# Channel attention in a fused gated layer stack: the bias products of the projections moved to 32 rows of the array, behind a slot's scores

## The chip, the cores and the metric

The kernel runs on one core of a Trainium2 chip. The metric is the device time of one execution, in microseconds. A core has a matmul engine (TensorE, PE in the profile, with its weight loads shown apart as PEld), three engines for elementwise work (VectorE or DVE, ScalarE or ACT, GpSimd or POOL) and a queue engine for transfers (SyncE or SP). Matmuls write to PSUM, eight banks of 128 partitions by 2 KB; the other engines read them there.

## The reference

A stack of layers works on x (16 batches, 128 tokens, 256 features). The first layer, the only one that the change touches, is a cross attention over channels, with 16 heads of size 8:

```python
q = einsum('oc,bct->bot', Wq, target) + bq      # 128 x 256 for each batch
k = einsum('oc,bcs->bos', Wk, source) + bk
v = einsum('oc,bcs->bos', Wv, source) + bv
dot = einsum('bhdt,bhds->bhts', q, k) / sqrt(8)
mask = target_mask[:, :, :, None] * source_mask[:, :, None, :]
dot = mask * dot - (1.0 - mask) * NEG
amap = softmax(dot, axis=-1) * mask
out = einsum('bhts,bhds->bhdt', amap, v)
```

Behind it come a feed-forward layer with ternary weights, two attentions over tokens, and a layer of routed experts. All of it is float32.

## The kernel before

`attend_channels` is the first stage, up to about 340 us of the execution. The other stages follow in blocks of their own.

**Layout.** A projection gives for each head 32 rows: the 8 rows of q (or k) three times, for a product in high and low parts, and a few rows that carry bias and mask terms. Four heads fill 128 partitions, so a head's scores contract over 32 rows only: partitions 32r to 32r+31, row group r. q and k of a batch are 512 rows each, made in two pieces of 256 (`part` 0 and 1), each piece in one PSUM bank (`proj`, two banks taken in turn) as two halves j of 128 x 256. v is one piece. So a batch has five pieces, q0, q1, k0, k1, v0.

**A piece.** `project` (L831) makes each half with four matmuls over the full array: the bias product, whose operands `bext` (bias rows) and `mext` (mask rows) are zero but for 4 of their 128 partitions (0 to 3), and three with high and low parts of weights and input. `project_v` (L849) does the same with the operands' roles exchanged. `freed` makes the piece wait until the piece two back has left its bank. ScalarE then rounds the piece out of its bank (`round_piece`, L744), and VectorE stacks the result (`stack_piece`, L1010), which frees the bank.

**Slots.** The order of all engines is written out by slots t; u = t mod 16. In slot t the first pass takes head u of batch t // 16: `first` (L872), two matmuls of 32 rows by 128 columns by 256, then VectorE's row maxima (L1019). The second pass runs 24 slots later: `second` (L892), two such matmuls with the maxima folded in, then ScalarE's exponential (L774). `first` of slot u uses row group u mod 4, `second` of the same slot group (u + 2) mod 4. In the stream of PE the two are interleaved: first 0, second 0, first 1, second 1. `first` waits for a free bank of three (the maxima of some slots before), `second` for one of two banks (the exponential of two slots before) and, at the first head of a batch, for the maxima that come back by DMA (L597).

At u = 0, 4, 8, 12 and 13 PE then makes a piece of the next batch (`built`, `PIECES`), at u = 2, 6, 10, 14 it weighs the values (`weigh`, L922, 128 rows by 32 columns), and at u = 2 it turns the maxima (L902). In the slots before 24 there is no second pass, and PE has other products of a later stage between (L151). In the slots -16 to -1 there are no scores at all, only batch 0's pieces. From slot 240 on no pieces are left.

ScalarE's order in a slot: the exponential, then at u = 2 the maxima (L760), at u = 1, 5, 9, 13 a piece's rounding, at 14 v (L750), at 0 a normalisation for a later batch (L727), at 3 the mask (L766), at 3 and 11 the outputs (L782).

Of the kernel before, what the change touches and what calls it, by code (L numbers as in the profile page):

```python
# [7 lines left out]
F32 = mybir.dt.float32  # L8
# [7 lines left out]
P = 128  # L16
# [350 lines left out]
def attend_channels(nc, res, io, gate, work, tern):  # L367

    x_sb, ident = res["x"], res["ident"]
    with ExitStack() as stack:  # L370
# [39 lines left out]
        mT = s.sb("mT", [A_HEADS, 2, DIM], F32R)  # L410
        PR = 8
        prob = s.sb("prob", [P, PR, 2, DIM])
        early = prob[0:4, :, :, :].rearrange("p a t n -> p (a t n)")
        braw, bhi = early[:, 0:1152], early[:, 1152:2304].bitcast(F32R)
        osb = s.sb("osb", [P, 2, A_TILES, DIM])
        num, den = (wraw[:, 512 * k:512 * k + 512].rearrange("p (b n) -> p b n", b=2) for k in range(2))
# [48 lines left out]
        def turned(t):  # L465

            b = t // U - 1
            return b if t % U == 2 and 0 <= b < BATCHES else None
# [27 lines left out]
        def prepared(t):  # L496

            b = t // U + 2
            return b if 2 <= b < BATCHES else None

        PIECES = {0: ("q", 0), 4: ("q", 1), 8: ("k", 0), 12: ("k", 1), 13: ("v", 0)}
        WARM = 40
        MEASURED, CONDENSED = 4, 17
# [67 lines left out]
        with nc.Block() as block:  # L571

            @block.sync
            def _(sp):
                lo, rest = slice(0, FIRST), slice(FIRST, BATCHES)
                sp.dma_start(x_sb[:, lo, :], io["x"][lo].rearrange("b p n -> p b n")).then_inc(ld_x[0], 16)
                sp.dma_start(wraw[:, 0:512], io["a_wq4"]).then_inc(ld_w, 16)
                sp.dma_start(wraw[:, 512:1024], io["a_wk4"]).then_inc(ld_w, 16)
                sp.dma_start(wraw[:, 1024:1152], io["a_wv"]).then_inc(ld_w, 16)
                sp.dma_start(cst[:, :], io["a_consts"]).then_inc(ld_w, 16)  # L580
                sp.dma_start(g[:, :], gate.broadcast_to([P, 1])).then_inc(ld_g, 16)
                sp.wait_ge(m_parts, 1)
                sp.wait_ge(blank_ext, 2)
                for k in range(4):
                    sp.dma_start(mext[k:k + 1, :].rearrange("o (b n) -> o b n", n=DIM).bitcast(F32),
                                 mparts[BATCHES * k:BATCHES * k + BATCHES, :].bitcast(F32)).then_inc(m_ext, 16)
                work.fetch(sp, 0)
                sp.dma_start(x_sb[:, rest, :], io["x"][rest].rearrange("b p n -> p b n")).then_inc(ld_x[1], 16)
                sp.dma_start(ctx_sb[:, rest, :], io["ctx"][rest].rearrange("b p n -> p b n")).then_inc(ld_c[1], 16)
                sp.dma_start(tm[:, rest, :].rearrange("p b n -> p (b n)"),  # L590
                             io["mask"][:, FIRST * DIM:].broadcast_to([P, (BATCHES - FIRST) * DIM])).then_inc(ld_m[1], 16)

                def maxima(b):
                    sp.wait_ge(mT_ready, b + 1)
                    for r in range(A_SLOTS):
                        row = A_ROWS * r + 27
                        sp.dma_start(qs[row:row + 1, b % A_BUFS, :, :].bitcast(F32),  # L597
                                     mT[A_TILES * r:A_TILES * r + A_TILES, b % 2, :].bitcast(F32))\
                            .then_inc(m_in[b % 2], 16)

                def gather(b):
                    p, i = b % 2, b // 2
                    sp.wait_ge(out_copied, 2 * b + 2)
                    if b >= 2:
                        sp.wait_ge(moved[p], 32 * i)
                    send(sp, p, 0)
                    if b < BATCHES - 1:
                        send(sp, p, 1)
                    sp.wait_ge(sent[p], 128 * (i + 1))
                    after(sp, x_done, 3 * (b - 1))  # L610
                    sp.dma_start(num[:, p, :], heads[p, 0]).then_inc(moved[p], 16)
                    if b < BATCHES - 1:
                        sp.dma_start(den[:, p, :], heads[p, 1]).then_inc(moved[p], 16)

                maxima(0)
                maxima(1)
                for b in range(BATCHES):
                    gather(b)
                    if b + 2 < BATCHES:
                        maxima(b + 2)  # L620
                    if b == 10:
                        sp.wait_ge(cm_ready, BATCHES)
                        work.fetch(sp, 1)
                    if b == 12:
                        sp.wait_ge(v_psum, BATCHES)
                        sp.wait_ge(tgm_ready, 14)
                        tern.load(sp)
# [197 lines left out]

            @block.tensor
            def _(pe):
                def project(b, kind, part, j):
                    psum_s, k = (q_psum, 0) if kind == "q" else (k_psum, 1)
                    h, l = ((xh, xl), (ch, cl))[k]  # L830
                    if j == 0:  # L831
                        freed(pe, b, kind, part)
                        pe.wait_ge((xl_ready, cl_ready)[k], b + 1)
                        if b == 0 and k == 0 and part == 0:
                            pe.wait_ge(w_lo, 1)
                            pe.wait_ge(b_ext, 1)
                            pe.wait_ge(m_ext, 64)
                    c = 512 * k + P * (2 * part + j)
                    w = slice(c, c + P)
                    o = proj[bank_of(b, kind, part)][:, j, :]  # L840
                    pe.matmul(o, bext[:, w], mext[:, DIM * b:DIM * b + DIM], start=True, stop=False)
                    pe.matmul(o, wh[:, w], h[:, b % 2, :], start=False, stop=False)
                    pe.matmul(o, wh[:, w], l[:, b % 2, :], start=False, stop=False)
                    mm = pe.matmul(o, wl[:, w], h[:, b % 2, :], start=False, stop=True)
                    if j == 1:
                        mm.then_inc(psum_s, 1)

                def project_v(b):
                    freed(pe, b, "v", 0)  # L849
                    w = slice(1024, 1152)  # L850
                    for t in range(2):
                        c = slice(P * t, P * t + P)
                        o = proj[bank_of(b, "v", 0)][:, t, 0:P]
                        pe.matmul(o, mext[:, DIM * b + P * t:DIM * b + P * t + P], bext[:, w], start=True, stop=False)
                        pe.matmul(o, ch[:, b % 2, c], wh[:, w], start=False, stop=False)
                        pe.matmul(o, ch[:, b % 2, c], wl[:, w], start=False, stop=False)
                        mm = pe.matmul(o, cl[:, b % 2, c], wh[:, w], start=False, stop=True)
                    mm.then_inc(v_psum, 1)

                def first(b, u, t):  # L860
# [74 lines left out]
                for t in SLOTS:  # L935
                    one, two = unit1(t), unit2(t)
                    for c in range(2):
                        if one:
                            first(*one, c)
                        if two:  # L940
                            second(*two, c)
                    if turned(t) is not None:
                        turn_maxima(turned(t))
                    if weighed(t):
                        weigh(*weighed(t))
                    u, b = t % U, built(t)
                    if b is not None:
                        if u in (0, 4, 8, 12):
                            project(b, *PIECES[u], 0)
                            project(b, *PIECES[u], 1)  # L950
                        if u == 13:
                            project_v(b)
                    if t in SUMMED:
                        pe.wait_ge(mT_ready, BATCHES)
                        tern.weight_sum(pe, SUMMED.index(t), side)
                    if t == TURNED:
                        tern.turn_scale(pe, 0, tern.sparts, scales, tern.FIRST, ident)
                    i, turns = gram_of(t)
                    for h in turns:
                        if h == 0:  # L960
                            gram_room(i)
                        work.multiply(pe, i, h, gram_bank[i])
# [5 lines left out]
            def _(dve):  # L968
# [11 lines left out]
                def mean_bias(a, b, k):  # L980
# [16 lines left out]
                dve.wait_ge(b_hi, 1)  # L997
                dve.wait_ge(ld_b, 16)
                dve.wait_ge(blank_ext, 2)
                dve.scalar_tensor_tensor(bext[0:4, :], bhi[:, :].bitcast(F32), ecst[0:4, 0:1], braw[:, :],  # L1000
                                         ALU.mult, ALU.add).then_inc(b_ext, 1)
                dve.wait_ge(vT_blank, 1)
                dve.memset(vT[:, :, :, :, A_HD:2 * A_HD], 1.0).then_inc(ones_set, 1)
# [2622 lines left out]
def lay_out(inputs):  # L3626
# [26 lines left out]
    bv[:3] = f["L0_xattn_bv"]  # L3653
    out["a_bias"] = np.concatenate([rows.reshape(4, -1), bv], 1)
    out["a_econsts"] = np.zeros((4 * BATCHES, 2), np.float32)
    out["a_econsts"][2, 0] = out["a_econsts"][BATCHES:2 * BATCHES, 1] = -1.0
    c = np.zeros((A_ROWS, 2), np.float32)
    c[[*range(16, 24), 26], 0] = -1.0
    c[[*range(8, 16), 25], 1] = -1.0
# [82 lines left out]
```

## Time and profile before

| | |
|---|---|
| median of 3 runs | 1811.39 us (1809.07 to 1817.93) |
| the profiled execution | 1818.41 us, its span 1816.6 us |
| busy, share of the span | PE 95%, PEld 80%, DVE 63%, ACT 54%, POOL 29% |
| mean granted clock of TensorE | 0.967 |
| the stage that changes | to about 340 us; pieces under scores from 28 to 275 us |

Times in the profile are microseconds from the start of the span. A matmul's row in the timeline has its start, its duration, the line, then output<-inputs, rows*columns of the array and the shape (partitions x elements). Durations overlap, since matmuls are pipelined; the distance between starts is what one costs in a stream. A matmul that has to wait for its own weights starts with their load. Rows that follow each other closely with the same line are merged (x2, x4).

### The profile page before, as it was taken

How to read it: one execution, taken by the hardware profiler on the slowest of the kernel's cores; microseconds unless marked ns; L12 is line 12 of the kernel's file. 1: busy time of each engine (PE TensorE's matmuls, PEld its weight loads, DVE VectorE, ACT ScalarE, POOL GpSimd, SP SyncE). 2: the span in 40 equal slices, each digit the busy share in tenths (PEclk: the TensorE clock that was granted, in tenths of full speed). 3: DMA queues.
4: the chain of work that ended last, by engine and by line, in shares of the span. 5: the costliest groups of instructions: out<-in, count | busy, mean ns of one | idle time of the engine just before them, and what ended most of it. 6: DMA issues, size and time to landing. Idle time of an engine off the chain costs nothing. (4 is left out here: it accounts for less than half of the span.)

```text
span 1816.6 us, 34407 instructions
## 1 busy us (share of the span) xinstructions
PE 1730.8 (95%) x11806; PEld 1449.5 (80%) x11814; DVE 1145.4 (63%) x2572; ACT 979.7 (54%) x2544; POOL 535.2 (29%) x578
## 2 busy tenths in 40 slices
PE   8999999698999999999999999999999998899997
PEld 6666665355888888888888888888888888789985
DVE  6788987687655656556556655555555566864434
ACT  2578886386554544454555555445445543755543
POOL 4233323153431211111112211111111211377773
PEclk9899998698999999999999999999999997999999
DMA  5011123012100100100001020101000004443447
GB/s 202 14 37 32 33 83 100 21 48 97 50 13 1 48 12 1 49 12 12 25 24 36 13 63 13 36 1 36 12 1 12 1 1 109 148 113 117 128 127 263
DMA packets 48775, 97.43 MB, mean 54 GB/s; under 512 B 7322, under 2 KB 29002, under 8 KB 47620
## 3 DMA queue, kind: packets, MB, share of 16 engines
q1 hardware_dynamic: 39807, 72.42, 13.1%
q0 software_dynamic: 7584, 21.37, 4.0%
q8 instruction: 104, 1.70, 0.4%
q10 hardware_dynamic: 1216, 1.41, 0.2%
q14 instruction: 64, 0.52, 0.1%
HBM read 73.85 MB, written 20.97 MB: 52 GB/s over the span
## 5 line engine op out<-in xcount | busy, mean ns | idle before, releaser
L2192 POOL TENSOR_TENSOR hold_wq<-hold_wq,ca_rsum 128x512 f32<-128x512 f32 x128 | 133.2, 1041 | 797.9 <-DVE ca_rsum L2434 797.9
L2046 ACT ACTIVATE hold_wq<-hold_wq,ca_nb,ca_evens 128x128 f32<-128x128 f32 x256 | 123.3, 483 | 227.5 <-DVE ca_nb L2429 227.5
L2046 ACT ACTIVATE hold_wq<-hold_wq,ca_nb,c_rqs 128x128 f32<-128x128 f32 x256 | 123.4, 483 | 225.8 <-DVE ca_nb L2429 225.8
L1019 DVE TENSOR_REDUCE a_mx<-a_s 128x2 f32<-128x512 f32 x256 | 166.4, 682 | 43.4 <-PE a_s L872 40.6
L774 ACT ACTIVATE a_prob<-a_s 128x512 f32<-128x512 f32 x256 | 147.8, 601 | 65.5 <-PE a_s L892 62.0
L2209 PE MATMUL ca_qk<-early_x,cw_wqkv_h 128*128 128x512 f32 x384 | 161.9, 422 | 1.0 <-PEq L1455 1.0
L2211 PE MATMUL ca_qk<-early_x,cw_wqkv_l 128*128 128x512 f32 x384 | 151.7, 395 | 0.0
L2210 PE MATMUL ca_qk<-early_x,cw_wqkv_h 128*128 128x512 f32 x384 | 151.2, 394 | 0.0
L2330 PE MATMUL ca_acc<-ca_wo_h,ca_oT_h 128*128 128x256 f32 x512 | 146.0, 285 | 0.0
L2331 PE MATMUL ca_acc<-ca_wo_l,ca_oT_h 128*128 128x256 f32 x512 | 145.0, 283 | 0.0
L2332 PE MATMUL ca_acc<-ca_wo_h,ca_oT_l 128*128 128x256 f32 x512 | 144.9, 283 | 0.0
L2252 PE MATMUL ca_s<-ca_qk 128*128 128x128 f32 x1024 | 135.7, 275 | 5.2 <-issue 5.2
L2271 PE MATMUL ca_oT<-hold_wq,ca_values 128*128 128x128 f32 x1024 | 136.1, 276 | 0.0
L2252 PEld LDWEIGHTS ca_s<-ca_qk 128*128 128x128 f32 x1024 | 125.3, 191 | 7.2 <-issue 7.0
L2434 DVE RECIPROCAL ca_rsum<-ca_sums 128x4 f32<-128x4 f32 x128 | 22.8, 178 | 167.3 <-ACT hold_wq L2046 167.3
L2271 PEld LDWEIGHTS ca_oT<-hold_wq,ca_values 128*128 128x128 f32 x1024 | 125.2, 193 | 0.0
L2424 DVE TENSOR_TENSOR hold_wq<-ca_s,hold_wk 128x512 f32<-128x512 f32 x128 | 88.1, 688 | 54.2 <-PE ca_s L2252 53.8
L892 PE MATMUL a_s<-a_qs,a_ks 32*128 32x256 f32 x512 | 102.6, 346 | 16.7 <-ACT a_prob L774 14.7
L2441 DVE SCALAR_TENSOR_TENSOR ca_oT_l<-ca_oT,ca_bv,ca_oT_h 128x512 fp32r<-128x512 f32 x64 | 48.1, 751 | 92.6 <-ACT ca_oT_h L2060 92.6
L2330 PEld LDWEIGHTS ca_acc<-ca_wo_h,ca_oT_h 128*128 128x128 f32 x512 | 97.7, 191 | 5.1 <-DVE ca_oT_l L2443 0.2
L2331 PEld LDWEIGHTS ca_acc<-ca_wo_l,ca_oT_h 128*128 128x128 f32 x512 | 97.4, 190 | 5.2
L2332 PEld LDWEIGHTS ca_acc<-ca_wo_h,ca_oT_l 128*128 128x128 f32 x512 | 97.4, 190 | 0.0
(526 smaller groups left out, 4893.0 us busy)
## 6 DMA issues: line engine op xcount, KB each, us to landing
early_big<-slot_results SPq DMA_DIRECT2D x16, 512.0 KB, 8.0
mw_raw<-in_d_expert_w SPq DMA_DIRECT2D x12, 352.0 KB, 5.3
a_heads<-a_osb SPq DMA_DIRECT2D x124, 32.0 KB
a_wraw<-a_heads SPq DMA_DIRECT2D x31, 128.0 KB, 2.1
mw_down<-in_d_expert_d SPq DMA_DIRECT2D x1, 2816.0 KB
token_rows<-early_rows SPq DMA_DIRECT2D x1, 2176.0 KB, 13.1
hold_wk<-in_c_wkT SPq DMA_DIRECT2D x1, 2064.0 KB
hold_wq<-in_c_wqT SPq DMA_DIRECT2D x1, 2064.0 KB, 8.0
```

What stands on the lines that cost most here:

```text
L774: act.activation(prob[:, w % PR, :, :], s2_bank(w)[:, :, :], ACT.Exp, scale=1.0 / A_ROOT)\
L1019: dve.tensor_reduce(mx[:, b % 2, :, h], s1_bank(b, u)[:, :, :], AX.X, ALU.max)\
L2046: ins = act.activation(prob[:, p, b, :], prob[:, p, b, :], ACT.Exp, bias=nb[:, p, b:b + 1], scale=row_scale[layer][:, r:r + 1], accum_out= ...
L2192: pool.tensor_tensor(prob[:, k % 2, :, :], prob[:, k % 2, :, :], rsum[:, k % 2, :].unsqueeze(2).broadcast_to([P, GB, TOKENS]), ALU.mult)\
L2209: pe.matmul(out, ah, bh, start=start, stop=False)
L2210: pe.matmul(out, ah, bl, start=False, stop=False)
L2211: return pe.matmul(out, al, bh, start=False, stop=stop)
L2252: mm = pe.matmul(s_ps[:, b, :], qk[:, p, 0, tok], qk[:, p, 1, tok], start=True, stop=True)
L2271: mm = pe.matmul(oT_ps[:, b, :], v[:, g_ % 2, b, c], pT[:, p, b, :], start=True, stop=True)
L2330: pe.matmul(acc[:, b, :], ah, bh, start=(h == 0 and b % 2 == 0), stop=False, skip_group_check=True)
L2331: pe.matmul(acc[:, b, :], ah, bl, start=False, stop=False, skip_group_check=True)
L2332: mm = pe.matmul(acc[:, b, :], al, bh, start=False, stop=(h == 3), skip_group_check=True)
```

## The change

The bias products leave `project` and `project_v`. A new function `bias` makes both of a piece's bias products directly behind the slot's scores, ahead of anything else of the slot. Its operands lie in partitions 32 to 35, and the matmuls read 32 partitions (32 to 63, row group 1) instead of 128: the form of the scores. The first of the two opens the accumulation for the whole bank (`start`), the second and the six matmuls of the piece add to it. The wait for the bank (`freed`) goes with them, ahead of the bias products; the wait for the low part of the input stays ahead of the six. The rest moves the operands: `bext`, `mext`, the bias constants and the scratch rows `early` go from partitions 0 to 3 to partitions 32 to 35.

```diff
-        early = prob[0:4, :, :, :].rearrange("p a t n -> p (a t n)")
+        early = prob[A_ROWS:A_ROWS + 4, :, :, :].rearrange("p a t n -> p (a t n)")
...
+        EXT = slice(A_ROWS, 2 * A_ROWS)
...
-                    sp.dma_start(mext[k:k + 1, :].rearrange("o (b n) -> o b n", n=DIM).bitcast(F32),
+                    sp.dma_start(mext[A_ROWS + k:A_ROWS + k + 1, :].rearrange("o (b n) -> o b n", n=DIM).bitcast(F32),
...
+                def bias(b, kind, part):
+                    freed(pe, b, kind, part)
+                    if b == 0 and kind == "q" and part == 0:
+                        pe.wait_ge(b_ext, 1)
+                        pe.wait_ge(m_ext, 64)
+                    o = proj[bank_of(b, kind, part)]
+                    for j in range(2):
+                        if kind == "v":
+                            pe.matmul(o[:, j, 0:P], mext[EXT, DIM * b + P * j:DIM * b + P * j + P], bext[EXT, 1024:1152],
+                                      start=(j == 0), stop=False, skip_group_check=True)
+                        else:
+                            c = 512 * (kind == "k") + P * (2 * part + j)
+                            pe.matmul(o[:, j, :], bext[EXT, c:c + P], mext[EXT, DIM * b:DIM * b + DIM],
+                                      start=(j == 0), stop=False, skip_group_check=True)
...
                 def project(b, kind, part, j):
...
                     if j == 0:
-                        freed(pe, b, kind, part)
                         pe.wait_ge((xl_ready, cl_ready)[k], b + 1)
                         if b == 0 and k == 0 and part == 0:
                             pe.wait_ge(w_lo, 1)
-                            pe.wait_ge(b_ext, 1)
-                            pe.wait_ge(m_ext, 64)
...
-                    pe.matmul(o, bext[:, w], mext[:, DIM * b:DIM * b + DIM], start=True, stop=False)
-                    pe.matmul(o, wh[:, w], h[:, b % 2, :], start=False, stop=False)
-                    pe.matmul(o, wh[:, w], l[:, b % 2, :], start=False, stop=False)
-                    mm = pe.matmul(o, wl[:, w], h[:, b % 2, :], start=False, stop=True)
+                    pe.matmul(o, wh[:, w], h[:, b % 2, :], start=False, stop=False, skip_group_check=True)
+                    pe.matmul(o, wh[:, w], l[:, b % 2, :], start=False, stop=False, skip_group_check=True)
+                    mm = pe.matmul(o, wl[:, w], h[:, b % 2, :], start=False, stop=True, skip_group_check=True)
...
                 def project_v(b):
-                    freed(pe, b, "v", 0)
...
-                        pe.matmul(o, mext[:, DIM * b + P * t:DIM * b + P * t + P], bext[:, w], start=True, stop=False)
...
+                    u, b = t % U, built(t)
+                    if b is not None and u in PIECES:
+                        bias(b, *PIECES[u])
                     if turned(t) is not None:
                         turn_maxima(turned(t))
                     if weighed(t):
                         weigh(*weighed(t))
-                    u, b = t % U, built(t)
```

## Rows read from the trace of the kernel before

**Rows 1.** The page: busy time, share of the span and instructions.

```profile
PE 1730.8 (95%) x11806; PEld 1449.5 (80%) x11814; DVE 1145.4 (63%) x2572; ACT 979.7 (54%) x2544; POOL 535.2 (29%) x578
```

**Rows 2.** Windows: length, busy of each engine, granted clock, DMA.

```profile
58.70:72.40 13.70, 13.70 (x91) 9.07 (x90) 6.38 (x10) 5.93 (x12) 3.55 (x6) 0.50 0.01 2
88.60:104.50 15.90, 15.52 (x171) 10.57 (x170) 14.25 (x23) 12.99 (x27) 5.67 (x10) 1.00 0.16 36
```

**Rows 3.** Waits, 27 to 300 us: us in total, times, longest.

```profile
ACT a_prob L774 <- PE a_s L892: 58.1, 87, 2.5
```

**Rows 4.** Timeline of PE, slot 12: last scores, piece k1, next scores.

```profile
111.69 0.38 PE L892 MATMUL a_s<-a_qs,a_ks 32*128 32x256 f32 x1 [0.25 <-ACT a_prob L774]
...
111.91 0.28 PE L892 MATMUL a_s<-a_qs,a_ks 32*128 32x256 f32 x1
112.11 0.39 PE L841 MATMUL a_proj<-a_mext,a_bext 128*128 128x256 f32 x1
112.34 0.28 PE L842 MATMUL a_proj<-a_ch,a_wh 128*128 128x256 f32 x1
112.45 0.27 PE L843 MATMUL a_proj<-a_cl,a_wh 128*128 128x256 f32 x1
...
113.04 0.28 PE L844 MATMUL a_proj<-a_ch,a_wl 128*128 128x256 f32 x1
113.25 0.38 PE L872 MATMUL a_s<-a_ks,a_qs 32*128 32x256 f32 x1
```

**Rows 5.** Timeline of PE, slots 15 and 0, and piece q0.

```profile
116.15 0.38 PE L872 MATMUL a_s<-a_ks,a_qs 32*128 32x256 f32 x1
...
116.17 0.38 PE L892 MATMUL a_s<-a_qs,a_ks 32*128 32x256 f32 x1
116.38 0.28 PE L872 MATMUL a_s<-a_ks,a_qs 32*128 32x256 f32 x1
...
116.39 0.28 PE L892 MATMUL a_s<-a_qs,a_ks 32*128 32x256 f32 x1
116.66 0.39 PE L841 MATMUL a_proj<-a_mext,a_bext 128*128 128x256 f32 x1
```

**Rows 6.** Timeline of PE: `second` of slot 25, `first` of slot 27, both group 3.

```profile
56.26 0.28 PE L892 MATMUL a_s<-a_qs,a_ks 32*128 32x256 f32 x1
...
56.38 0.27 PE L872 MATMUL a_s<-a_ks,a_qs 32*128 32x256 f32 x1
```

**Rows 7.** Timeline of PE, slots 7 and 8, and piece k0.

```profile
107.72 0.38 PE L892 MATMUL a_s<-a_qs,a_ks 32*128 32x256 f32 x1
...
107.94 0.36 PE L892 MATMUL a_s<-a_qs,a_ks 32*128 32x256 f32 x2
...
108.14 0.27 PE L892 MATMUL a_s<-a_qs,a_ks 32*128 32x256 f32 x1
108.34 0.39 PE L841 MATMUL a_proj<-a_mext,a_bext 128*128 128x256 f32 x1
```

**Rows 8.** Timeline of ScalarE, slots 15 to 6.

```profile
117.69 0.60 ACT L727 ACTIVATE a_xn<-x_sb,a_nbias,a_rstd 128x256 f32<-128x256 f32 x1
118.37 0.60 ACT L774 ACTIVATE a_prob<-a_s 128x512 f32<-128x512 f32 x1
118.87 0.59 ACT L744 ACTIVATE a_hi<-a_proj 128x512 fp32r<-128x512 f32 x1
...
121.55 1.19 ACT L774 ACTIVATE a_prob<-a_s 128x512 f32<-128x512 f32 x2
```

**Rows 9.** Timeline of PE's weight loads, slot 6.

```profile
122.20 0.18 PEld L892 LDWEIGHTS a_s<-a_qs,a_ks 32*128 32x128 f32 x1 [0.33 <-ACT a_prob L774]
```

**Rows 10.** Timeline of VectorE: two stacks that free a bank.

```profile
24.32 0.75 DVE L1010 SCALAR_TENSOR_TENSOR a_qs<-a_hi,a_cst,a_proj 128x512 fp32r<-128x512 f32 x1 [0.89 <-ACT a_hi L744]
...
115.87 0.74 DVE L1010 SCALAR_TENSOR_TENSOR a_ks<-a_hi,a_cst,a_proj 128x512 fp32r<-128x512 f32 x1
```

**Rows 11.** The tile a_proj, 27 to 300 us: duration ns min/median/max, first and last start.

```profile
L841 PE MATMUL a_proj<-a_mext,a_bext x120: 278/382/581, 28.1 to 272.9; 128*128 128x256 f32 x120
```

More of the change, by code:

```diff
@@ L853, in project_v @@
                         o = proj[bank_of(b, "v", 0)][:, t, 0:P]
-                        pe.matmul(o, mext[:, DIM * b + P * t:DIM * b + P * t + P], bext[:, w], start=True, stop=False)
-                        pe.matmul(o, ch[:, b % 2, c], wh[:, w], start=False, stop=False)
-                        pe.matmul(o, ch[:, b % 2, c], wl[:, w], start=False, stop=False)
-                        mm = pe.matmul(o, cl[:, b % 2, c], wh[:, w], start=False, stop=True)
+                        pe.matmul(o, ch[:, b % 2, c], wh[:, w], start=False, stop=False, skip_group_check=True)
+                        pe.matmul(o, ch[:, b % 2, c], wl[:, w], start=False, stop=False, skip_group_check=True)
+                        mm = pe.matmul(o, cl[:, b % 2, c], wh[:, w], start=False, stop=True, skip_group_check=True)
                     mm.then_inc(v_psum, 1)
@@ L999, in _ @@
                 dve.wait_ge(blank_ext, 2)
-                dve.scalar_tensor_tensor(bext[0:4, :], bhi[:, :].bitcast(F32), ecst[0:4, 0:1], braw[:, :],
+                dve.scalar_tensor_tensor(bext[A_ROWS:A_ROWS + 4, :], bhi[:, :].bitcast(F32),
+                                         ecst[A_ROWS:A_ROWS + 4, 0:1], braw[:, :],
                                          ALU.mult, ALU.add).then_inc(b_ext, 1)
@@ L3655, in lay_out @@
     out["a_econsts"] = np.zeros((4 * BATCHES, 2), np.float32)
-    out["a_econsts"][2, 0] = out["a_econsts"][BATCHES:2 * BATCHES, 1] = -1.0
+    out["a_econsts"][A_ROWS + 2, 0] = out["a_econsts"][BATCHES:2 * BATCHES, 1] = -1.0
     c = np.zeros((A_ROWS, 2), np.float32)
```

## The prediction

> **What bounds the kernel now.** First the page's busy times: TensorE's matmuls fill 95% of the span [rows 1], so the first question is what its stream loses in the stage that changes. That stage is the channel attention, 27 to 340 us. Second, the stretch by stretch table [rows 2]: in one batch period (15.9 us at the full clock, 16 slots) PE is busy 15.52 us, VectorE 14.25 and ScalarE 12.99. All three are close to full, so a matmul saved counts only where PE is the one that the others wait for at that moment. Third, the waits [rows 3]: ScalarE waits 58.1 us in this stage for scores (L892 to L774), 87 times, so there are such moments, about six in a period. Fourth, the order of single instructions around each projection piece, which says at which of the five pieces of a period that is so.
>
> The full-array piece, at slot 12 (k, part 1) [rows 4]: scores at 111.69 and 111.91, first projection matmul (the bias product, L841) at 112.11, the next at 112.34, the third at 112.45, the eighth at 113.04, the next scores at 113.25. So: from the last 32-row score to the first full-array matmul 0.20 us; first to second 0.22 (the weights of the first are loaded in the open); each further one 0.12; back to the scores 0.21. The two bias products of a piece are two links of 0.12 in this chain.
>
> **What the change takes away.** In each q or k piece eight full-array matmuls become six: 2 x 0.12 = 0.24 us less. The exposed first weight load stays, because L842 then stands first. In the v piece likewise two links, of about 0.11 us. There are no more switches between the 32-row form and the full array than before where scores stand ahead of the piece, since bias products now follow scores in the scores' form and no other matmul comes between.
>
> **What it adds.** Two 32-row matmuls in row group 1 (partitions 32 to 63). What they cost is a question of which row groups are busy. At slots 0, 4, 8 and 12 the slot's own scores use groups 0 and 2, and the slot before used groups 3 and 1 (its `second` sits in group 1). At slot 13 `first` uses group 1 itself.
>
> Do row groups run beside each other, and out of the program's order? The tight case, slots 15 and 0 [rows 5]: eight scores, four start at 116.15 to 116.17, four at 116.38 to 116.39. In the program the second half of slot 15 (same row groups as its first half) stands ahead of the first half of slot 0; if starts kept the order, slot 0 could not start beside slot 15. So a row group is a line of its own: 0.22 us from its first matmul after a break to its second, and 0.12 to a third behind it (56.26 to 56.38, group 3) [rows 6].
>
> The Trainium skill says otherwise (PSUM — Partial Sum Buffer, section Engine vs sequencer instructions): matmuls "start and complete in program order", with only weight loads pulled ahead. This trace doesn't agree for starts in different row groups, by the four starts within 0.02 us. By the page's rule the total below would be near -0.5 us, by the rows -4.4; it is rival B.
>
> Now the five pieces of a period:
>
> - Slot 12. The scores of slot 12 come late, behind the exponential (0.25 us idle), at 111.69 and 111.91 [rows 4]; group 1 has long been empty. The two bias products are issued behind them and run beside them. Cost 0 in the forecast, 0.12 if starts keep their order. Net -0.24. On the path: ScalarE and VectorE wait for slot 13's scores.
> - Slot 8. Scores of slot 7 in group 1 at 107.72 and 107.94, the last score of slot 8 at 108.14, bias at 108.34 [rows 7]. Bias products at 107.94 + 0.12 = 108.06 and 108.18, projection at 108.18 + 0.20 = 108.38 in place of 108.34: +0.04. Net -0.20. On the path, as slot 9's scores are what ScalarE waits for next.
> - Slot 4. As slot 12: -0.24 on PE. But behind it ScalarE is in an unbroken run, from 118.37 on to the pair of exponentials at 121.55, and PE itself then waits 0.33 us for it, at 122.20 [rows 8, 9]. The gain turns into a longer wait there. Worth 0.
> - Slot 0. The piece waits for its bank, which VectorE's stack of k (L1010) frees at 115.87 + 0.74 = 116.61 [rows 10]; the bias product starts 0.05 later, at 116.66, and not 0.20 behind the last score (116.39) but 0.27 [rows 5]. After the change this wait stands ahead of the 32-row pair, which has nothing left to hide behind: pair 0.22 (first start to second), 0.20 for the switch, so the projection starts 0.42 later, less 0.24: net +0.18. On the path: the exponential at 118.37 waits for slot 1's scores, while the operation before it (L727, 117.69) would let ScalarE on 0.48 after its start, some 0.2 us earlier (its usual pace: 0.50 from the exponential at 118.37 to the operation behind it) [rows 8].
> - Slot 13, v. Group 1 holds two scores of its own; third and fourth matmul in it cost 2 x 0.12, two links of 0.11 are saved: 0.
>
> Sum of a period: +0.18 - 0.20 - 0.24 = -0.26 us. Twelve periods look like this (slot 0 pieces from 84.84 to 260.98 us): -3.1 us.
>
> Ahead of them, 27 to 81 us (the bias products of the q and k pieces under scores run from 28.1 to 272.9, 120 of them, two to a piece [rows 11]): only first-pass scores run up to 54 us, group 1 is free at slots 0, 4, 8, 12, so a piece gains 0.24. I count five such pieces on the path (28.14, 31.84, 40.82, 50.75, 54.89): -1.2; one hidden behind VectorE (35.98): 0; one that waits for VectorE (45.84): +0.2. The one at 58.66 falls where the clock is half [rows 2] and a link about twice 0.12: -0.4. Of the next, two tight ones give 0 (66.56, 72.42), then -0.1 and -0.24 (76.52, 80.29). Together -1.75.
>
> The opening, 19.8 to 27.7 us: batch 0's pieces have no scores ahead of them. There the change does add switches: k part 1 starts at 25.12 because VectorE's stack of q (24.32 + 0.75) frees its bank [rows 10]. As at slot 0 the pair then stands alone, +0.18; the same for k part 0 and v. The bias product of q part 0 moves ahead of the wait for the lowered x and gains 0.4, which the new switches of q part 1 take back. Together +0.5.
>
> Other edits: operands at partitions 32 to 35 in place of 0 to 3 have the same sizes, so VectorE's and ScalarE's instructions and the four DMAs into the mask rows cost what they cost; they end by about 18 us, ahead of the first projection at 19.87. If that cover were gone they would move the opening one to one.
>
> By the Trainium skill (TensorEngine Tiling (Array Packing), section Key Properties) a change of the tiling mode drains the array. The trace agrees: 0.20 in place of 0.12. By that rule too the two bounds of a piece differ only in whether a switch is added, which happens in the opening alone.
>
> **Sum.** -3.1 - 1.75 + 0.5 = -4.4 us, all within the stage; behind it the stages follow one another, so it reaches the end one to one. The profiled execution took 1818.4 us (span 1816.6 and 1.8 around it) and would take 1814.0. It was 7.0 us above the median of the runs, 1811.39. I carry the difference, not the level: 1811.4 - 4.4 = 1807.0. The three runs lie 8.9 us apart, so about 0.5% (9.06 us) is what can be told from no change.
>
> **Rivals.**
>
> A, all the PE time counts. ScalarE's run at slots 1 to 6 gives way too, and the pair at slot 0 hides: 12 x 3 x 0.24 + 1.75 = 10.4 less, and the opening's loss hidden too: 1801.0, 0.57% faster. For it: PE's 95% [rows 1]. Against it: PE's own wait at 122.20 [rows 9].
>
> B, starts keep the program's order (the page's rule). The pair then ends 0.12 behind the last score: slot 12 -0.12, slot 8 about -0.11, slot 0 still +0.18; a period -0.05, twelve of them -0.6; ahead of them six times -0.12 and +0.2; opening +0.5. About -0.6: 1810.8.
>
> C, the slower side: the clock. The granted clock is 0.50 in 58.7 to 72.4, behind two waits of PE for the exponentials, and 1.00 through the batch periods [rows 2]. At 0.50 it issued 91 matmuls in 13.7 us; at 1.00 171 take 15.9, so 91 take 8.5: a stretch costs 5.2 us. Each period loses 10 full-array matmuls of some 171 and gets longer waits at slots 4 to 6. If the clock fell in these periods it would take three more such stretches to undo 4.4 and cost over 9: (9.06 + 4.4) / 5.2 = 2.6. With three: 1822.6. Against: periods with 0.33 us waits and gaps held 1.00.
>
> D, the pair never overlaps: 0.24 each, so pieces break even, and slot 0 and the opening lose: 12 x 0.18 + 0.2 + 0.5 = +2.9: 1814.3. It would need group 1 to be blocked by the other groups, which [rows 5] speaks against.
>
> **Chances and range.** Forecast 0.50, A 0.13, B 0.16, C 0.09, D 0.12. The likeliest one's own range is 1803 to 1811. From 1801 (A's value) to 1816 (D with a run's scatter) 0.8 and a bit lies; outside are most of C, and A where it scatters lower. Faster by over 0.5%: A, with a little of the forecast's scatter, 0.14; slower by over 0.5%: C, 0.08; within: 0.78.
>
> **What would show it.** In the changed trace: six full-array matmuls per piece, piece length 0.90 in place of 1.14. At slot 12 two 32-row bias matmuls that start with the scores, and 0.20 from the last score to the projection; at slot 8 some 0.04 later than now; at slot 0 bias products 0.05 behind VectorE's stack and the projection 0.42 behind their first. The wait at 122.20 grows to about 0.5. Period 15.65 us in place of 15.9. Wrong it would be if bias products start only behind the last score (B), if the periods shrink by 0.7 (A), or if the granted clock has new stretches of 0.50 (C), which could also hide or double the gain by where the stretch at 58.7 falls.

## The result: slower by 0.6%, with a stage that gains where it was forecast and loses its clock where it was not

The changed kernel's median is 1824.51 us (20 runs, 1811.55 to 1832.93), that of the kernel before 1812.8 (20 runs, 1807.0 to 1817.93): ratio 1.0062, 95% interval 1.0049 to 1.0076. Forecast were 1807.0 us and a range of 1801 to 1816. The profiled execution took 1832.93 us, span 1831.0. It is the slowest of the 20: the comparison of the two traces shows what the change does to the clock at its fullest, the medians what it costs in general.

The page of the changed kernel first, part 1 and the clock's row of part 2 (each digit a fortieth of the span, 46 us), then the clock's row of the kernel before:

```profile
PE 1743.4 (95%) x11806; PEld 1453.3 (79%) x11814; DVE 1149.3 (63%) x2572; ACT 979.0 (53%) x2544; POOL 533.5 (29%) x578
PEclk6599999688999999999999999999999997899999
```
```profile
PEclk9899998698999999999999999999999997999999
```

The same number of matmuls (x11806, as in [rows 1]), shares that agree within a point, and two lower digits at the very start. The windows of the changed kernel say how long that lasts (columns as in [rows 2]):

```profile
20.00:25.00 5.00, 4.92 (x17) 4.02 (x18) 1.04 (x2) 1.19 (x2) 3.58 (x7) 0.50 1.10 351
...
30.00:40.00 10.00, 10.00 (x37) 6.79 (x36) 4.41 (x8) 2.07 (x4) 3.56 (x6) 0.50 0.04 17
...
16.20:91.30 75.10, 71.31 (x288) 48.57 (x288) 39.66 (x78) 18.13 (x36) 18.30 (x28) 0.50 0.20 73
91.30:104.50 13.20, 12.55 (x147) 8.43 (x139) 10.33 (x17) 10.00 (x21) 0.82 (x2) 1.00 0.12 22
```

and the same windows of the kernel before:

```profile
20.00:25.00 5.00, 5.00 (x24) 4.87 (x24) 1.43 (x2) 1.20 (x2) 3.35 (x6) 0.54 1.10 349
...
30.00:40.00 10.00, 9.79 (x51) 6.29 (x51) 9.40 (x19) 1.20 (x2) 2.38 (x5) 1.00 0.04 14
```

Before, the granted clock is 0.50 (1.2 GHz) from 17.8 to 24.6 us, rises to 1.00 (2.4 GHz) in the opening, and falls once more among the pieces, from 58.8 to 72.4. After, it is 0.50 from 16.2 to 91.3 us without a break. Behind the last piece both fall again (301.1 to 338.6 and 316.6 to 343.9 us); all that lies behind it changes the difference of the two spans by 0.4 us only (below).

The first fall is there in both: PE has nothing to do from 13.7 us (13.0 in the changed kernel) until the opening's first matmul, and the clock falls within that gap. What brings it back in the kernel before is the opening. Its q0 and q1 are 16 full-array matmuls on end, about 0.21 us apart; here are the first and the last:

```profile
19.87 0.58 PE L841 MATMUL a_proj<-a_mext,a_bext 128*128 128x256 f32 x1 [6.15 <-POOL a_xl L652]
...
23.24 0.41 PE L844 MATMUL a_proj<-a_xh,a_wl 128*128 128x256 f32 x1
```

Two places divide the two traces into three parts. The last matmul of the v piece of slot 45 starts at 82.70 before and 101.92 after, the last of the stage's last piece at 274.75 and 289.56 (in this order, before's two and after's two):

```profile
82.70 0.27 PE L857 MATMUL a_proj<-a_wh,a_cl 128*128 128x128 f32 x1
...
274.75 0.27 PE L857 MATMUL a_proj<-a_wh,a_cl 128*128 128x128 f32 x1
```
```profile
101.92 0.27 PE L867 MATMUL a_proj<-a_wh,a_cl 128*128 128x128 f32 x1
...
289.56 0.28 PE L867 MATMUL a_proj<-a_wh,a_cl 128*128 128x128 f32 x1
```

So +19.2 us up to slot 45 (forecast: -1.75 + 0.5, with a little more of it behind 82 us), then -4.4 us in the twelve periods (forecast -3.1), together +14.8; the spans differ by 14.4. The periods gained more than I said. The stretch ahead of them has 75.1 us at half rate against 6.8 + 13.7 = 20.5, so 54.6 us more. If its other terms came to the -1.25 of the forecast, the clock took 19.2 + 1.25 = 20.5 us, 0.37 us for each us at 0.50. My price, 5.2 us for 13.7, was 0.38.

**The pieces, one by one**, in the changed kernel's timeline of PE. Slot 8 (L902 is `second`, L882 `first`, L841 the bias product, L854 the first projection matmul):

```profile
189.84 0.39 PE L902 MATMUL a_s<-a_qs,a_ks 32*128 32x256 f32 x2
...
189.96 0.29 PE L841 MATMUL a_proj<-a_mext,a_bext 32*128 32x256 f32 x1
190.08 0.28 PE L902 MATMUL a_s<-a_qs,a_ks 32*128 32x256 f32 x1
190.09 0.27 PE L841 MATMUL a_proj<-a_mext,a_bext 32*128 32x256 f32 x1
190.29 0.38 PE L854 MATMUL a_proj<-a_ch,a_wh 128*128 128x256 f32 x1
...
191.19 0.38 PE L882 MATMUL a_s<-a_ks,a_qs 32*128 32x256 f32 x1
```

The first bias product starts at 189.96, ahead of the slot's last score at 190.08, which stands ahead of it in the program; the projection starts 0.21 behind that score, as if the pair weren't there. Piece 0.90 instead of 1.15. From the last score to the next scores it is 1.11 us (190.08 to 191.19), where it was 1.35 (108.14 in [rows 7] to 109.49): -0.24, where I had -0.20. Slot 12:

```profile
193.39 0.38 PE L902 MATMUL a_s<-a_qs,a_ks 32*128 32x256 f32 x1
...
193.40 0.38 PE L841 MATMUL a_proj<-a_mext,a_bext 32*128 32x256 f32 x1
193.61 0.27 PE L902 MATMUL a_s<-a_qs,a_ks 32*128 32x256 f32 x1
193.62 0.28 PE L841 MATMUL a_proj<-a_mext,a_bext 32*128 32x256 f32 x1
193.83 0.38 PE L854 MATMUL a_proj<-a_ch,a_wh 128*128 128x256 f32 x1
...
194.74 0.38 PE L882 MATMUL a_s<-a_ks,a_qs 32*128 32x256 f32 x1
```

The pair runs with the scores, 0.01 behind each. From the last score to the next scores it is 1.13 us, where it was 1.34 (111.91 to 113.25 in [rows 4]): -0.21. Slot 0, where VectorE's stack (first fence) frees the bank (PSUM is read here by VectorE and ScalarE, not by every engine):

```profile
197.30 0.74 DVE L1023 SCALAR_TENSOR_TENSOR a_ks<-a_hi,a_cst,a_proj 128x512 fp32r<-128x512 f32 x1
```
```profile
182.94 0.39 PE L854 MATMUL a_proj<-a_xh,a_wh 128*128 128x256 f32 x1
...
198.09 0.50 PE L841 MATMUL a_proj<-a_mext,a_bext 32*128 32x256 f32 x2
198.52 0.39 PE L854 MATMUL a_proj<-a_xh,a_wh 128*128 128x256 f32 x1
```

The stack ends at 198.04, the pair starts 0.05 later, the projection 0.43 behind it (forecast 0.42). From 182.94 to 198.52 is a period: 15.58 us, where it was 15.91. And slot 6, which waits for the exponential, in the weight loads' timeline:

```profile
188.19 0.18 PEld L902 LDWEIGHTS a_s<-a_qs,a_ks 32*128 32x128 f32 x1 [0.51 <-ACT a_prob L775]
```

0.51 us, where [rows 9] had 0.33: most of slot 4's gain has become a wait.

**The opening**, changed kernel, clock at 0.50:

```profile
21.32 0.41 PE L856 MATMUL a_proj<-a_xh,a_wl 128*128 128x256 f32 x1
21.67 0.79 PE L841 MATMUL a_proj<-a_mext,a_bext 32*128 32x256 f32 x2
22.39 0.58 PE L854 MATMUL a_proj<-a_xh,a_wh 128*128 128x256 f32 x1
22.77 0.41 PE L855 MATMUL a_proj<-a_xl,a_wh 128*128 128x256 f32 x1
```

Six full-array matmuls, then 21.32 to 22.39, 1.07 us, of a switch (to the 32-row form), the pair and a switch back, and so on between all pieces. Before, the 16 of q0 and q1 were unbroken. That is the trace's hint at the cause. A hint is all it is: the changed kernel is also short of ten full-array matmuls there, and has 32-row pairs in slots 0 to 31, and each of these could be what keeps the clock down.

### The profile page after: what moved, and what is told of

Its sections match the earlier page's. It is cut to its first block and busy times, and to the rows that moved or that the text cites. A ratio compares the mean times of both kernels' runs of the same rounds, so it can differ in the third digit from the quotient of the medians.

```text
span 1831.0 us, 34345 instructions
## 1 busy us (share of the span) xinstructions
PE 1743.4 (95%) x11806; PEld 1453.3 (79%) x11814; DVE 1149.3 (63%) x2572; ACT 979.0 (53%) x2544; POOL 533.5 (29%) x578
## 5 line engine op out<-in xcount | busy, mean ns | idle before, releaser
L902 PE MATMUL a_s<-a_qs,a_ks 32*128 32x256 f32 x512 | 104.8, 348 | 15.6 <-ACT a_prob L775 14.1
L882 PE MATMUL a_s<-a_ks,a_qs 32*128 32x256 f32 x512 | 103.3, 361 | 0.0
```

## The experiments

Most of them share one edit to the changed kernel, and differ in its condition:

```diff
                 def bias(b, kind, part):
                     freed(pe, b, kind, part)
...
+                    rows = EXT if CONDITION else slice(0, P)
                     o = proj[bank_of(b, kind, part)]
...
-                            pe.matmul(o[:, j, :], bext[EXT, c:c + P], mext[EXT, DIM * b:DIM * b + DIM],
+                            pe.matmul(o[:, j, :], bext[rows, c:c + P], mext[rows, DIM * b:DIM * b + DIM],
```

Where the condition doesn't hold, the bias products stand at the new place but use the full array. Ratios are against the kernel before on the same chip (its medians there 1810.99, 1811.25 and 1811.94 us in the three groups of four). Times are medians; a ratio is worked out from the runs of the two kernels taken together and can differ a little from the quotient of two medians. Windows quoted below are the runs' profiled executions, columns as in [rows 2]; the first of the last three numbers is the granted clock. A table behind the runs has the stretches of 0.50 of each trace and the mean clock of all executions.

**e1_open_full**, condition `b > 0`.

> The changed kernel, but batch 0's five pieces (the opening, no scores ahead of them) take their bias products over the full array again; all other pieces keep the 32-row pair. Theory T1: in the changed kernel the opening no longer brings the granted clock back to 1.00 at 24.6 us (it stays 0.50 from 16.2 to 91.3), because the change breaks the unbroken run of full-array matmuls there; the batch periods themselves gain (15.58 us in place of 15.91). Then the clock rises near 24.6 us here, the stretch of 0.50 up to 91 us is gone, and the time is 4 to 6 us below the kernel before: ratio 0.997 to 0.998. Rival T2: the 32-row pairs behind the scores, from 28 us on, keep the clock low; then the clock stays 0.50 to about 90 us here too and the ratio is near 1.006. Rival T3: both places matter: the clock rises at 24.6 but falls again between 28 and 80 us for longer than before's 13.7 us; ratio 0.999 to 1.004.

Measured: 1806.35 us, ratio 0.9978 (0.9955 to 1.0001).

```profile
25.00:30.00 5.00, 4.96 (x31) 3.85 (x31) 2.88 (x4) 2.07 (x5) 1.93 (x4) 1.00 1.07 409
...
40.00:60.00 20.00, 20.00 (x68) 13.55 (x66) 11.29 (x32) 3.04 (x6) 5.74 (x7) 0.50 0.01 2
```

The clock rose at 23.0 us, as T1 said. In the profiled execution (1813.43 us, one of the slower of its ten) it fell again from 40.1 to 81.1, which T1 did not say and T3 did; the ratio is in T1's range and below T3's. It is -4.0 us (-8.1 to +0.2) for everything outside the opening, where the prediction had -3.1 - 1.75 = -4.9.

**e2_open_only**, condition `b == 0`: the opening alone has pairs.

> The converse: only batch 0's pieces use 32 rows; the bias products of all other pieces stand at the new place, but over the full array (the pair, then six matmuls, eight in one run). T1: the clock stays 0.50 from about 17 us on, well past 58 us; ratio 1.005 to 1.012, as the gain of the periods is missing too. T2: the clock rises near 24.6 us as before; ratio 0.999 to 1.001. T3: rises, but somewhat later than 24.6; ratio about 1.002 to 1.005.

Measured: 1820.17 us, ratio 1.0064 (1.0043 to 1.0085). This is +11.6 us (7.8 to 15.4; 9.2 by the medians) for five pairs in the opening, where the prediction had +0.5. The whole change costs 11.2 by its ratio, but has the gains of the periods in it, which e2 has not.

```profile
20.00:25.00 5.00, 4.71 (x17) 3.81 (x17) 0.83 (x2) 1.19 (x2) 3.77 (x7) 0.50 1.10 352
...
30.00:40.00 10.00, 10.00 (x36) 7.45 (x36) 4.62 (x8) 1.47 (x3) 3.54 (x6) 0.50 0.04 15
```

0.50 from 17.3 to 41.2 in the trace, a run of 1813.53 us and a mean clock of 0.971; its other nine took 1811 to 1826 us at 0.963 to 0.972, so how long the clock stays down varies from execution to execution. The ratio is in T1's range, and T2 falls. That the clock would stay down well past 58 us, as T1 had it, this trace doesn't show.

**e3_after_warm** and **e4_before_warm**: `WARM` 66 in place of 40 (the identity products that fill the time ahead of the first piece), in the changed kernel and in the one before.

```diff
-        WARM = 40
+        WARM = 66
```

> The changed kernel with 66 in place of 40 idle-time transposes of the identity ahead of the first piece, so that the array is in use up to about 18.9 us and the clock should still be 1.00 when the opening begins. T1 (the clock is the loss, not the pairs): with the clock at 1.00 through the opening the time falls to 4 to 8 us below the kernel before, ratio 0.995 to 0.998. T2: the clock falls between 28 and 90 us all the same; ratio 1.003 to 1.006. T3: rises or holds at first, falls at about 58 us for some 14 us as before; ratio 0.996 to 1.000.

> The kernel before with the same 66. It shows what the filled gap alone brings: all theories expect the first stretch of 0.50 (17.8 to 24.6 us) to vanish, worth at most 3 us, ratio 0.998 to 1.000. The difference between this and the changed kernel with 66 is the change at equal clock: by my terms -0.26 to -0.33 us in twelve periods and -1.75 ahead of them, 4 to 5 us; by T2 the changed one stays slower.

Measured: the changed kernel 1811.6 us, ratio 1.0003 (0.9972 to 1.0034), its ten runs from 1800.97 to 1823.03; the kernel before 1807.03, ratio 0.9981 (0.9964 to 0.9998). In this order, 20 to 25 and 30 to 40 us of the changed one, then of the one before:

```profile
20.00:25.00 5.00, 4.74 (x22) 3.75 (x22) 1.49 (x2) 1.19 (x2) 3.71 (x7) 0.72 1.10 353
...
30.00:40.00 10.00, 10.00 (x34) 6.64 (x32) 4.89 (x8) 1.57 (x3) 3.55 (x6) 0.50 0.08 32
```
```profile
20.00:25.00 5.00, 4.11 (x32) 3.70 (x31) 2.10 (x3) 2.07 (x4) 3.28 (x6) 1.00 1.10 353
...
30.00:40.00 10.00, 9.79 (x52) 6.63 (x52) 9.77 (x20) 1.19 (x2) 1.00 (x2) 0.98 0.06 23
```

The stretch of 0.50 ahead of the opening is gone in both, as expected: it came from the gap. My expectation for the changed one, T1's ratio, was wrong. In its profiled execution (1822.81 us) the clock is 1.00 when the opening begins, and falls in it, at 22.2 us; before's opening holds it, and the clock falls at 39.5 us for 10 us. So in that trace an opening with pairs doesn't keep the clock. In other executions it seems to: five of the ten have a mean clock of 0.971 to 0.973 and took 1801 to 1811 us, the other five 0.960 to 0.966 and 1813 to 1823.

**e5_late_pairs**, condition `b > 2`, and **e6_late_pairs_q0_full**, condition `b > 2 and (kind, part) != ('q', 0)`.

> The changed kernel with full-array bias products for batches 0, 1 and 2, so in the opening and in slots 0 to 31; 32-row pairs only from slot 32 on. Where the first experiments stand: with the full-array form in the opening alone the clock rose at 23 us but was 0.50 again from 40.1 to 81.1; with 32 rows in the opening alone it was 0.50 from 17.3 to 41.2. Theory T3 (both places matter, because each takes full-array matmuls out of a stretch where the clock is near falling): here the stretches of 0.50 are those of the kernel before, about 18 to 25 and 59 to 72 us, the periods are 15.58 us each, and the ratio is 0.997 to 0.998. Rival (the clock is lost through the pairs in the batch periods too, or by chance): a low stretch of over 25 us between 40 and 100, ratio at or above 0.999.

> As the one before, and the first piece of each batch (q part 0, slot 0) keeps its bias products over the full array for all batches, since there the wait for the bank leaves the 32-row pair nothing to hide behind (0.43 us from its start to the projection, two links of 0.12 saved). By my terms 0.18 us a period: period 15.40 in place of 15.58, twelve or thirteen periods, 2.2 us less than the one before; ratio 0.996 to 0.997. Rival: slot 0's piece is not on the path, since ScalarE has a run of its own behind it: period stays 15.58.

Measured: 1808.92 us, ratio 0.9988 (0.9970 to 1.0006), stretches of 0.50 at 16.0 to 26.2 and 60.4 to 70.6; and 1804.96 us, ratio 0.9960 (0.9943 to 0.9976), stretches at 16.9 to 23.8 and 40.8 to 51.1. The first gained less than I expected, though the expected 0.998 lies within its interval; the stretches are about where they were before. The second is the test of slot 0: giving the pair up where it had nothing to hide behind brings the period from 15.58 to 15.43 us, 0.15, where my term was 0.18. Its rival, that slot 0 isn't on the path, falls.

**e7_pair_and_full** and **e8_neither**: for batches 0 to 2, both forms, or no bias product at all.

```diff
-                    for j in range(2):
+                    for rows, j in [(r, j) for r in ((EXT,) if b > 2 else (EXT, slice(0, P))) for j in range(2)]:
...
```

```diff
+                    if b <= 2:
+                        return
                     for j in range(2):
...
-                    pe.matmul(o, wh[:, w], h[:, b % 2, :], start=False, stop=False, skip_group_check=True)
+                    pe.matmul(o, wh[:, w], h[:, b % 2, :], start=(b <= 2), stop=False, skip_group_check=True)
```

> For batches 0, 1 and 2 both forms: the 32-row pair, whose result is thrown away (the full-array pair behind it opens the accumulation anew), and then the full run of eight. From slot 32 on as in the changed kernel. Ta, the clock is lost through the two full-array matmuls that each piece is short of: here none is missing, so the stretches of 0.50 are as with the full form alone, and only the pairs and switches cost, some 2 to 3 us; ratio 0.998 to 1.000. Tb, it is lost through the pair and its switches between the forms: the clock stays low to 40 us or longer, ratio 1.003 or more.

> Batches 0, 1 and 2 leave the bias products out altogether (their outputs lack bias and mask terms); from slot 32 on as in the changed kernel. Ta: six full-array matmuls in a row and nothing else, so the clock is lost as in the changed kernel: 0.50 for 24 us or more in all before 100 us, beyond the stretches of 18 to 25 and 59 to 72; ratio 1.000 to 1.006 although work is left out. Tb: no pairs and no added switches, so the clock is as before; ratio 0.996 to 0.998.

Measured: with both 1817.51 us, ratio 1.0026 (1.0004 to 1.0048); with neither 1802.84 us, ratio 0.9955 (0.9933 to 0.9978). First both, then neither:

```profile
20.00:25.00 5.00, 5.00 (x19) 4.10 (x19) 0.79 (x2) 1.19 (x2) 3.39 (x6) 0.50 1.10 350
...
30.00:40.00 10.00, 10.00 (x38) 7.33 (x38) 3.97 (x6) 1.84 (x4) 3.54 (x6) 0.50 0.04 16
```
```profile
20.00:25.00 5.00, 4.55 (x21) 4.14 (x22) 1.49 (x2) 1.53 (x3) 3.47 (x6) 0.60 1.10 349
...
30.00:40.00 10.00, 9.55 (x49) 6.05 (x49) 9.97 (x20) 1.19 (x2) 1.66 (x3) 1.00 0.04 14
```

With all full-array matmuls there and the 32-row pairs between them, the clock stays 0.50 from 15.2 to 42.5 us. With ten full-array matmuls fewer in the opening and nothing between the rest, it is 1.00 again at 24.0. Ta (matmuls missing) falls, Tb (the pair and its switches) stands. Both ratios miss Tb's narrowly (1.003 or more, 0.996 to 0.998). Which part of Tb does it, the small matmuls or the time that the switches take from the full-array ones, isn't shown: every run with the pairs has both. The busy column doesn't tell: PE is busy 5.00 of 5.00 us where the clock stays low and 4.55 where it rises.

**e9_first_pair_only**, condition `b > 0 or (kind, part) == ('q', 0)`, and **e10_four_pairs**, condition `b > 0 or (kind, part) != ('q', 0)`.

> In the opening only the first pair, that of q part 0, uses 32 rows (it stands ahead of the wait for x, some 1 us before the first projection); the other four pieces of batch 0 are full-array; from slot 0 on as in the changed kernel. What stands so far: the clock is lost where the opening's pieces have the pair and its switches between them, not where full-array matmuls are only missing. If it is the switches between pieces that keep the clock at 0.50 (Tb1), this one rises near 23 to 25 us, as q part 0 and 1 make an unbroken run of 14 full-array matmuls: ratio 0.996 to 0.999. If the pair's mere presence ahead of the run does it (Tb2), 0.50 lasts past 40 us, ratio 1.002 or more.

> The converse: q part 0 of batch 0 over the full array, the other four pieces of the opening with the 32-row pair. Tb1: the switches stand between all pieces, 0.50 from about 17 to past 40 us, ratio 1.004 to 1.008. Tb2: rises near 24 us, ratio 0.997 to 1.000.

Measured: 1807.79 us, ratio 0.9986 (0.9972 to 1.0000), the clock back at 23.9 us; and 1818.05 us (8 runs), ratio 1.0036 (1.0007 to 1.0065), a little under the 1.004 of Tb1, 0.50 from 17.9 to 69.1 and again from 75.9 to 93.0. A pair ahead of the run does no harm that these runs can tell, pairs between the pieces do (Tb1). The timeline of the first one, with the run that it keeps (14 full-array matmuls, from 20.04 to 22.98):

```profile
20.04 0.58 PE L855 MATMUL a_proj<-a_xh,a_wh 128*128 128x256 f32 x1 [1.05 <-POOL a_xl L653]
...
21.28 0.41 PE L857 MATMUL a_proj<-a_xh,a_wl 128*128 128x256 f32 x1
21.49 0.63 PE L842 MATMUL a_proj<-a_mext,a_bext 128*128 128x256 f32 x2
21.92 0.42 PE L855 MATMUL a_proj<-a_xh,a_wh 128*128 128x256 f32 x1
...
22.98 0.41 PE L857 MATMUL a_proj<-a_xh,a_wl 128*128 128x256 f32 x1
```

and its links show the clock: 0.21 us up to 22.98, and 0.12 from 23.98 on:

```profile
23.98 0.28 PE L856 MATMUL a_proj<-a_cl,a_wh 128*128 128x256 f32 x1
24.10 0.28 PE L857 MATMUL a_proj<-a_ch,a_wl 128*128 128x256 f32 x1
```

**e11_best**, condition `b > 0 and (kind, part) != ('q', 0)`, and **e12_best_warm**, the same with `WARM` 66 as in e3.

> What the runs point to: batch 0's pieces and every batch's q part 0 over the full array, 32-row pairs everywhere else. The clock rises near 24 us; period 15.43 in place of 15.58 (changed) and 15.91 (before), 12 periods: 5.8 us, and some more ahead of them. Ratio 0.995 to 0.997, median 1802 to 1806. If 32-row pairs in slots 0 to 31 lengthen the second stretch of 0.50 (41 us in one trace of the version with the opening alone mended), it is 0.997 to 1.000, worse than the version with pairs from slot 32 on (0.996).

> The one before, with 66 in place of 40 transposes ahead of the first piece. The same 66 gave the kernel before 0.998 and spread the changed kernel between 1801 and 1823. With an opening that can hold the clock the two gains should add: ratio 0.993 to 0.996. If the clock falls again at some point between 22 and 60 us for long, as in the changed kernel with 66, 0.997 to 1.001.

Measured: 1803.81 us, ratio 0.9958 (0.9943 to 0.9973), and 1804.86 us, ratio 0.9953 (0.9935 to 0.9972). Two starts of the same v matmul in e11, one period apart, 15.43 us:

```profile
171.88 0.27 PE L868 MATMUL a_proj<-a_wh,a_cl 128*128 128x128 f32 x1
...
187.31 0.28 PE L868 MATMUL a_proj<-a_wh,a_cl 128*128 128x128 f32 x1
```

e11 is the version that the runs point to: 0.42% below the kernel before and some 1.0% below the changed one (0.9958 / 1.0062 = 0.990). The longer filling adds nothing that these runs can tell. (One execution of e12 took 5742 us; the ratio leaves it out, and without it the median is 1804.19.)

**All runs side by side.** The mean clock is the mean over all executions of a version, the stretches are those of its one trace; (66) is the longer filling ahead of the opening. The kernel before stands with its 97 executions beside the experiments, since for its first 20 only the times are on record.

| version | pairs between the opening's pieces | ratio | mean clock | 0.50 in the trace, up to 110 us |
|---|---|---|---|---|
| before | no | 1 | 0.972 | 17.8-24.6, 58.8-72.4 |
| e4 (66) | no | 0.9981 | 0.975 | 39.5-49.8 |
| e1 | no | 0.9978 | 0.969 | 16.2-23.0, 40.1-81.1 |
| e5 | no | 0.9988 | 0.971 | 16.0-26.2, 60.4-70.6 |
| e6 | no | 0.9960 | 0.972 | 16.9-23.8, 40.8-51.1 |
| e8 | no | 0.9955 | 0.970 | 17.2-24.0, 58.2-71.8 |
| e9 | no | 0.9986 | 0.970 | 17.1-23.9, 58.0-75.1 |
| e11 | no | 0.9958 | 0.971 | 16.3-23.1, 57.3-67.5 |
| e12 (66) | no | 0.9953 | 0.972 | 39.4-49.6, 59.9-70.1 |
| changed | yes | 1.0062 | 0.961 | 16.2-91.3 |
| e2 | yes | 1.0064 | 0.967 | 17.3-41.2 |
| e3 (66) | yes | 1.0003 | 0.967 | 22.2-70.0, 76.8-87.0 |
| e7 | yes | 1.0026 | 0.966 | 15.2-42.5, 69.8-80.0 |
| e10 | yes | 1.0036 | 0.963 | 17.9-69.1, 75.9-93.0 |

The clock of all executions, and not of one trace alone, divides the versions by the form of the opening: 0.961 to 0.967 with pairs between its pieces, 0.969 to 0.975 without.

## Why the prediction was wrong, by its own steps

**The step that failed** is the opening. I wrote that its pieces "have no scores ahead of them. There the change does add switches", priced them at +0.5 us as three pairs that stand alone, and went on. I had the right place and the right fact, and asked only what the switches cost by themselves. What they break is the run of full-array matmuls that brings the clock back to 1.00, and once that chance is missed, the stage runs at half rate for longer, to 41 us in e2's trace and to 91 in the changed kernel's. e2 shows the step by itself: five pairs in the opening, 1.0064, +11.6 us (7.8 to 15.4) where I had +0.5. e1 takes it out: 0.9978, -4.0 us, where my other terms came to -4.9. So the rest of the sum agrees with what e1 measured (-8.1 to +0.2), and the opening's term failed.

**Rival C** had the mechanism (the clock) and its price (0.38 us for each us at 0.50; 0.37 from the two traces), but the wrong place. That its 1822.6 lies near the measured 1824.51 is luck: three stretches were taken as the number that could be told from no change. I looked for new falls in the batch periods, where the clock held 1.00, and gave it 0.09. The trace of before had the right question in it: the clock was 0.50 at 20 us and rose during the opening. Of that I showed nothing ([rows 2] have the fall at 58.7 alone), and did not ask what raised it.

**The terms that held.** Slot 12: -0.21, forecast -0.24. Slot 8: -0.24, forecast -0.20. Slot 4: became a wait, 0.51 for 0.33 us. Slot 0: the pair's start to the projection 0.43, forecast 0.42; last score to next scores 1.59 us for 1.42, +0.17, forecast +0.18 (+0.15 by e6). Slot 13: last score to next scores 1.20 us for 1.24, -0.04, forecast 0. Together, with slot 4 at 0, -0.32; the period measured -0.33 us, forecast -0.26. The misses are slots 8 and 13, against them slot 12. **Rival B**, that matmuls start in the program's order, falls by the rows of slot 8. The prediction gives it -0.5 us in one place and -0.6 in another; its terms add up to -0.6. **Rival D**, no overlap, falls by the same rows, and **rival A**, all PE time counts, by slot 6's longer wait.

**What the spread says.** Among the changed kernel's 20 runs the fastest, 1811.55 us, has a mean granted clock of 0.968, the slowest, 1832.93, one of 0.955. Time at 0.50 is twice the share missing to 1: 2 x 0.032 x 1809.7 = 116 us and 2 x 0.045 x 1831.0 = 165 us; 49 us more at half rate for 21.4 us, 0.44 for each; a straight line through all 20 has 0.38. So most of the spread is how long the clock stays down. The same working over all executions gives 142 us at 0.50 for the changed kernel (mean clock 0.961) and 102 for the one before (0.972). At 0.38 the 40 us more are worth about 15 us. Measured were 11.2, so about 4 were gained elsewhere: an estimate, but it is what the forecast had without its opening, -4.9. At the same clock (0.967 and 0.968), the profiled execution before took 1818.41 us and the fastest after 1811.55; these are single runs, but they lie on the side of the forecast.

**What stays open.** Why the clock rises at 41 us in one trace and 91 in another, and why it fell at about 40 us in the traces of e1, e4, e6 and e12, but not in e9's, which has e1's matmuls from slot 0 on, or in e11's. One execution of each version was profiled. Whether it is the small matmuls or the switches in the opening isn't shown. Whether 32-row pairs behind the opening cost some clock can't be told by the ratios: e1 (with them) 0.9978, e5 (without those of slots 0 to 31) 0.9988. The clocks hint at it: e2's ten executions have 122 us at 0.50 on average, 20 more than the kernel before, the changed kernel's 40 more. So the opening alone may account for only half of the lost clock, and the pairs further on may keep it down once the opening has missed its rise.

## What to carry to other kernels

A change of shape on the matmul engine has two prices: the chain of starts, which a timeline gives to a hundredth of a microsecond, and the clock. Look up every place where the granted clock rises, ask which unbroken run raised it, and keep small-tile matmuls and switches out of that run. A form that is right in the steady state (small matmuls beside others of their form) can be wrong in a prologue, where it stands alone. And a matmul that moves ahead of a piece moves behind that piece's wait: where the wait is for another engine, it has nothing to hide behind.

## What the runs showed of the hardware that I had not expected

In these traces the clock rises in the opening's full-array run (24.6 us before, 23.0 to 26.2 in the six like it that began at 0.50) or holds there (e4, e12). With pairs of 32-row matmuls between the pieces it did neither in the five traces (changed, e2, e3, e7, e10), though PE counts as busy (5.00 of 5.00 us at 0.50 in e7; 4.55 of 5.00 in e8, where it rises). The Trainium skill (TensorE: Matmul & The Clock Gate, section What's actually happening) says that the clock starts throttled and activity releases it. The traces agree on the second half (0.50 after the gap that begins at 13.7 us, 1.00 again behind the full-array run); the start they don't show, the column has 1.00 from 0 us on.

A matmul in one row group overtook a matmul in another that stands ahead of it: 189.96 against 190.08 in slot 8. The same page of the Trainium skill (section The mechanism) has matmuls start and end in strict order; this trace shows otherwise for starts.

A switch between the 32-row form and the full array cost 0.20 to 0.22 us from start to start at full clock (193.61 to 193.83) and 0.35 at half (21.32 to 21.67), where a link within the full-array form cost 0.12 and 0.21.
